# A transformer block on one core: the attention's last product split into three fp32r products, with new instruction orders

## The reference, cut to what matters

```python
x  = L0_attn_x                                   # (8, 1024, 256) fp32, 8 batches
xn = layernorm(x)
# attention without softmax, 16 heads of depth 16
q = elu(xn @ Wq + bq) + 1 ;  k = elu(xn @ Wk + bk) + 1 ;  v = xn @ Wv + bv
k = k / sqrt(sum(k * k, head) + EPS)
attn = (q @ k.T) @ v                             # per head
a = layernorm(xn + attn @ Wo + bo) * gamma + beta
# feed-forward: three blocks with dequantised 4-bit weights and a low-rank addition
h = xn
for blk in range(3):
    y = gelu(layernorm(h @ W[2 * blk].T + b) * g + be)
    h = y @ W[2 * blk + 1].T + b + h
out = x + a + h
```

## Time and profile before

| | |
|---|---|
| median of 3 runs | 626.99 us (626.99 to 627.79) |
| profiled execution, its own time | 627.22 us |
| its span, first to last instruction | 625.5 us |
| TensorE busy | 597.2 us, 95% |
| VectorE busy | 489.4 us, 78% |
| ScalarE busy | 447.2 us, 71% |
| GpSimd busy | 377.6 us, 60% |
| granted TensorE clock, mean | 0.998 |

### The profile page before, as it was taken

One profiled execution on the slowest core, in us unless ns is written; L12 is line 12 of the kernel. 1 busy time (PEld: TensorE's weight loads), 2 busy tenths in 40 slices (PEclk: granted clock), 3 DMA queues, 4 the chain that ended last, 5 costly groups with the idle time before them and its releaser, 6 DMA issues.

```text
span 625.5 us, 10360 instructions
## 1 busy us (share of the span) xinstructions
PE 597.2 (95%) x3365; PEld 508.9 (81%) x3365; DVE 489.4 (78%) x1084; ACT 447.2 (71%) x699; POOL 377.6 (60%) x361
## 2 busy tenths in 40 slices
PE   7999999999998999989999999989999899999996
PEld 7887889878897788968798688977889687987885
DVE  3578679796897868888797968978688887976687
ACT  3367778677778597686796777785976867967752
POOL 3565666366655765466763666557654567626665
PEclk9999999999999999999999999999999999999999
DMA  8103000500004000320005000050003200040001
GB/s 256 42 9 129 0 1 35 168 2 2 0 35 168 0 0 0 116 85 0 0 0 201 0 0 0 34 168 0 0 0 124 78 0 0 0 136 0 2 1 68
DMA packets 11460, 29.01 MB, mean 46 GB/s; under 512 B 2592, under 2 KB 4272, under 8 KB 11440
## 3 DMA queue, kind: packets, MB, share of 16 engines
q1 hardware_dynamic: 10960, 28.35, 13.4%
q10 hardware_dynamic: 480, 0.41, 0.3%
HBM read 20.37 MB, written 8.39 MB: 46 GB/s over the span
## 4 chain that ended last, share of the span: by engine, by line
PE 64%; ACT 14%; POOL 8%; issue 7%; DVE 6%; DMA 1%; POOLq 0%; DVEq 0%; ACTq 0%
PE bank L1469 17%; PE bank L1475 8%; PE bank L1596 8%; PE bank L1640 6%; PE bank L1585 6%; ACT fw L630 5%; PE bank L1542 4%; PE bank L1561 3%; ACT gh L635 3%; POOL gl L262 2%; PE bank L1552 2%; PE bank L1569 2%; PE bank L1529 2%; ACT L630 2%; POOL XNB L412 2%
## 5 line engine op out<-in xcount | busy, mean ns | idle before, releaser
L262 POOL TENSOR_TENSOR gl<-fw,gh 128x512 fp32r<-128x512 f32 x80 | 104.6, 1320 | 74.6 <-ACT gh L635 74.5
L620 ACT ACTIVATE fw<-bank,b1c 128x512 f32<-128x512 f32 x96 | 62.2, 685 | 57.3 <-PE bank L1475 57.1
L417 POOL TENSOR_TENSOR sqs<-fw 128x512 f32<-128x512 f32 x48 | 62.6, 1303 | 63.6 <-ACT fw L620 63.2
L953 DVE SCALAR_TENSOR_TENSOR fw<-bank,b1c,rb 128x512 f32<-128x512 f32 x96 | 68.2, 744 | 18.7 <-ACT rb L626 18.7
L392 POOL TENSOR_TENSOR rsf<-vef,neghalf 128x4 f32<-128x4 f32 x48 | 49.5, 1032 | 52.0 <-DVE vef L944 51.1
L630 ACT ACTIVATE fw<-fw,vec 128x512 f32<-128x512 f32 x96 | 74.1, 808 | 7.1 <-DVE fw L953 5.9
L267 POOL TENSOR_TENSOR hTl<-hT,hTh 128x512 fp32r<-128x512 f32 x40 | 54.5, 1379 | 14.8 <-ACT hTh L639 14.4
L1596 PE MATMUL bank<-K,XN 128*128 128x256 f32 x256 | 60.7, 379 | 0.0
L1640 PE MATMUL bank<-M,qT 128*128 128x256 f32 x256 | 59.0, 379 | 0.0
L635 ACT ACTIVATE gh<-fw 128x512 fp32r<-128x512 f32 x96 | 56.8, 620 | 0.5
L392 POOL TENSOR_TENSOR rs<-ve,neghalf 128x2 f32<-128x2 f32 (+1 forms) x48 | 39.0, 816 | 23.6 <-DVE ve L1041 13.9
(11 more groups left out here) (155 smaller groups left out, 1586.9 us busy)
## 6 DMA issues: line engine op xcount, KB each, us to landing
X<-in_L_attn_x_dram SPq DMA_DIRECT2D x16, 512.0 KB, 6.0
RES<-in_L_attn_x_dram SPq DMA_DIRECT2D x16, 512.0 KB, 4.6
out_dram<-RES SPq DMA_DIRECT2D x14, 512.0 KB, 2.7
XNB<-in_L_ffn_qweights_dram SPq DMA_DIRECT2D x2, 512.0 KB, 6.9
out_dram<-RES SPq DMA_DIRECT2D x4, 256.0 KB, 2.1
RES<-in_L_ffn_qweights_dram SPq DMA_DIRECT2D x1, 512.0 KB, 7.6
Y<-in_L_ffn_lora_a_dram ACTq DMA_DIRECT2D x4, 96.0 KB, 5.1
Wp<-in_L_attn_Wk_dram SPq DMA_DIRECT2D x1, 256.0 KB, 5.3
```

What stands on the lines that cost most here:

```text
L262: engine.tensor_tensor(gl[:, h, m, :], fw[:, h, m, :], gh[:, h, m, :].bitcast(F32), ALU.subtract).then_inc(g_low[h][m], 1)
L417: pool.tensor_tensor(sqs[:, h, :], fw[:, h, 0, :], fw[:, h, 1, :], ALU.add).then_inc(sqs_ready[h], 1)
L620: act.activation(fw[:, h, m, :], FB[h][m][:], ACT.Square, bias=b1c[:, m, j:j + 1]).then_inc(sq_ready[h], 1)
L953: dve.scalar_tensor_tensor(fw[:, h, m, :], FB[h][m][:], b1c[:, m, j:j + 1], rb[:, h, :], ALU.add, ALU.mult).then_inc(yn_ready[h], 1)
```

## The change

1. qT becomes qTh and qTl, M becomes Mh and Ml, all fp32r. `q_elu` writes back to eq; the new `q_higher` (ScalarE) rounds eq to qTh, the new `q_lower` (GpSimd) makes qTl. `m_copy` writes Mh, the new `m_lower` (VectorE) makes Ml.
2. `attend` makes, for each row tile, six fp32r products in place of two in fp32, and waits for the low parts of q (q_low) and of M.
3. eq is free for the next `q_exp` of its column only after `q_lower`.
4. Space: the masked lora_b, lbT, moves into the buffers of sqs and eq, so the first `add_squares` waits until the weights' low parts 0 to 2 are made and the first `q_exp` until all are; the row of bv lies in BD in place of M.
5. New orders of all engines' queues and of the PSUM uses, in head, body and tail, and of the first loads.

```diff
+                if at == HEAD:
+                    act.wait_ge(wT_split, NL)
+                if h or at != HEAD:
+                    act.wait_ge(q_low[m], i * 2 + h)
                 act.activation(eq[:, m, :], RB[r][:], ACT.Exp, bias=neg1[:, 0:1]).then_inc(eq_ready, 1)
+            def q_higher(i, h, m):
+                act.wait_ge(q_ready, nth(i, 2 * NC, h * NC + m))
+                act.activation(qTh[m][:, half(h)], eq[:, m, :], ACT.Copy).then_inc(q_high, 1)
...
+            def q_lower(i, h, m):
+                pool.wait_ge(q_high, nth(i, 2 * NC, h * NC + m))
+                pool.tensor_tensor(qTl[m][:, half(h)], eq[:, m, :], qTh[m][:, half(h)].bitcast(F32), ALU.subtract
+                                   ).then_inc(q_low[m], 1)
...
             def add_squares(i, h, j):
+                if isinstance(i, int) and i == 0 and j == 0:
+                    pool.wait_ge(wT_split, 3)
...
-                dve.scalar_tensor_tensor(qT[m][:, half(h)], eq[:, m, :], 1.0, RB[r][:], ALU.min, ALU.max
+                dve.scalar_tensor_tensor(eq[:, m, :], eq[:, m, :], 1.0, RB[r][:], ALU.min, ALU.max
                                          ).then_inc(q_ready, 1)
+            def m_lower(i, at):
+                r, n = rotating(i, ("m",), at)
+                dve.wait_ge(m_high, nth(i, 1, 0))
+                dve.tensor_tensor(Ml[:].rearrange("p c d -> p (c d)"), RB[r][:],
+                                  Mh[:].rearrange("p c d -> p (c d)").bitcast(F32), ALU.subtract).then_inc(m_ready, 1)
...
             def attend(i, p, at):
                 r = take(i, ("out", p), at)
-                pe.wait_ge(q_ready, nth(i, 2 * NC, p // 2 * NC + NC - 1))
+                for m in range(NC):
+                    pe.wait_ge(q_low[m], nth(i, 2, p // 2))
                 pe.wait_ge(m_ready, nth(i, 1, 0))
+                pairs = [(q, w, c) for q, w in ((qTl, Mh), (qTh, Ml), (qTh, Mh)) for c in range(NC)]
                 for t in range(2):
-                    for c in range(NC):
-                        ins = pe.matmul(RB[r][:, t * D:(t + 1) * D], qT[c][:, (2 * p + t) * P:(2 * p + t + 1) * P],
-                                        M[:, c, :], start=(c == 0), stop=(c == NC - 1))
+                    for n, (q, w, c) in enumerate(pairs):
+                        ins = pe.matmul(RB[r][:, t * D:(t + 1) * D], q[c][:, (2 * p + t) * P:(2 * p + t + 1) * P],
+                                        w[:, c, :], start=(n == 0), stop=(n == len(pairs) - 1))
```

Of the new orders in the loop's body, those that the prediction speaks of, written short (behind a # the place in the queue):

```diff
 # GpSimd
+                q_lower(i, 0, 0)            # between add_squares(i, 0, 1) and add_squares(i, 1, 1)
+                q_lower(i, 1, 0)            # between ffn_root(i, 0, 1) and ffn_root(i, 1, 1)
+                q_lower(i, 0, 1)            # behind g_lower(i, 0, 1, 1)
+                q_lower(i, 1, 1)            # behind ffn_root(i, 0, 2)
-                base_xn(i, 0..3)            # behind ffn_root(1,0), ffn_root(0,1), h_lower(0,1,1), add_squares(1,2)
+                base_xn(i, 0..3)            # behind add_squares(0,0), add_squares(1,0), ffn_root(1,0), ffn_root(1,1)
 # TensorE
                 second_high(i, 1, 1, BODY)
+                make_m(i, BODY)
                 second_low(i, 1, 1)
-                make_m(i, BODY)
 # VectorE
                 q_elu(i, 1, 0, BODY)
+                k_hat(i, 2)
                 k_hat(i, 3)
                 ffn_var(i, 1, 1, BODY)
...
                 ffn_residual(i, 1, 1, 0, BODY)
+                m_lower(i, BODY)
                 ffn_residual(i, 1, 1, 1, BODY)
...
+                att_result(i, 0, BODY)
                 xt_lower(i + 1, 0, 0, BODY)
-                att_result(i, 0, BODY)
 # ScalarE
                 gelu(i, 1, 0, 0)
-                gelu(i, 1, 0, 1)
                 gelu(i, 0, 0, 1)
                 g_higher(i, 0, 0, 1)
+                gelu(i, 1, 0, 1)
...
+                m_copy(i, BODY)
                 q_exp(i, 1, 1, BODY)
-                m_copy(i, BODY)
```

More of the change, by code:

```diff
@@ L455, in head @@
                 dequantise(3)
-                qk_lower(1)
                 dequantise(4)
                 base_xn(0, 0, HEAD)
+                dequantise(5)
                 add_squares(0, 0, 0)
-                dequantise(5)
                 ffn_root(0, 0, 0)
+                qk_lower(1)
+                add_squares(0, 1, 0)
                 base_xn(0, 1, HEAD)
-                base_xn(0, 2, HEAD)
-                add_squares(0, 1, 0)
                 ffn_root(0, 1, 0)
@@ L473, in head @@
                 add_squares(0, 0, 1)
+                q_lower(0, 0, 0)
                 add_squares(0, 1, 1)
@@ L476, in head @@
                 ln1_root(1, 0)
+                q_lower(0, 0, 1)
                 ffn_root(0, 1, 1)
+                base_xn(0, 2, HEAD)
                 base_xn(0, 3, HEAD)
@@ L481, in head @@
                 g_lower(pool, 0, 1, 1, 1)
+                q_lower(0, 1, 0)
                 h_lower(pool, 0, 0, 1, 1)
@@ L484, in head @@
                 add_squares(0, 0, 2)
+                q_lower(0, 1, 1)
+                ffn_root(0, 0, 2)
                 ln2_root(0, 0)
-                ffn_root(0, 0, 2)
                 ln2_root(0, 1)
@@ L539, in tail @@
                 add_squares(i, 1, 0)
+                base_xn(i, 0, TAIL)
                 ffn_root(i, 1, 0)
+                base_xn(i, 1, TAIL)
                 g_lower(pool, i, 0, 0, 0)
@@ L547, in tail @@
                 h_lower(pool, i, 1, 0, 1)
+                q_lower(i, 0, 0)
                 add_squares(i, 0, 1)
-                base_xn(i, 0, TAIL)
+                add_squares(i, 1, 1)
                 ffn_root(i, 0, 1)
-                add_squares(i, 1, 1)
                 ffn_root(i, 1, 1)
+                q_lower(i, 1, 0)
+                base_xn(i, 2, TAIL)
                 g_lower(pool, i, 0, 1, 1)
+                q_lower(i, 0, 1)
                 g_lower(pool, i, 1, 1, 0)
                 g_lower(pool, i, 1, 1, 1)
+                base_xn(i, 3, TAIL)
                 h_lower(pool, i, 0, 1, 1)
-                base_xn(i, 1, TAIL)
+                q_lower(i, 1, 1)
                 add_squares(i, 0, 2)
-                base_xn(i, 2, TAIL)
                 ln2_root(i, 0)
@@ L563, in tail @@
                 ln2_root(i, 1)
-                base_xn(i, 3, TAIL)
                 ffn_root(i, 1, 2)
@@ L764, in head @@
                 ln1_normalise(1, 1, HEAD)
+                q_higher(0, 1, 1)
                 square(0, 1, 2, 0, HEAD)
@@ L806, in body @@
                 h_higher(i, 0, 0, 1)
-                q_exp(i, 0, 1, BODY)
+                q_higher(i, 0, 0)
                 h_higher(i, 1, 0, 0)
@@ L810, in body @@
                 square(i, 0, 1, 0, BODY)
-                q_exp(i, 1, 0, BODY)
                 square(i, 0, 1, 1, BODY)
+                q_exp(i, 0, 1, BODY)
                 square(i, 1, 1, 0, BODY)
                 square(i, 1, 1, 1, BODY)
+                q_exp(i, 1, 0, BODY)
+                q_higher(i, 0, 1)
+                q_higher(i, 1, 0)
                 rb_copy(i, 0, 1, BODY)
@@ L835, in body @@
                 xt_copy(i + 1, 0, 0, BODY)
+                q_higher(i, 1, 1)
                 square(i, 1, 2, 0, BODY)
@@ L1253, in head @@
                 ffn_residual(0, 1, 1, 0, HEAD)
+                m_lower(0, HEAD)
                 ffn_residual(0, 1, 1, 1, HEAD)
                 xt_lower(1, 0, 0, HEAD)
+                h_lower(dve, 0, 1, 1, 0)
                 h_lower(dve, 0, 1, 1, 1)
-                h_lower(dve, 0, 1, 1, 0)
+                q_elu(0, 1, 1, HEAD)
                 att_y(0, 0, HEAD)
@@ L1378, in tail @@
                 k_hat(i, 2)
+                k_hat(i, 3)
+                ffn_var(i, 1, 1, TAIL)
                 ffn_normalise(i, 0, 1, 0, TAIL)
-                ffn_var(i, 1, 1, TAIL)
-                k_hat(i, 3)
                 ffn_normalise(i, 0, 1, 1, TAIL)
@@ L1388, in tail @@
                 ffn_residual(i, 0, 1, 1, TAIL)
+                h_lower(dve, i, 0, 1, 0)
+                q_elu(i, 1, 1, TAIL)
                 ffn_residual(i, 1, 1, 0, TAIL)
                 ffn_residual(i, 1, 1, 1, TAIL)
-                h_lower(dve, i, 0, 1, 0)
-                q_elu(i, 1, 1, TAIL)
+                m_lower(i, TAIL)
                 h_lower(dve, i, 1, 1, 0)
@@ L1823, in head @@
                 spread_rstd(0, 0, 2, HEAD)
+                attend(0, 3, HEAD)
                 attend(0, 2, HEAD)
-                attend(0, 3, HEAD)
                 turn_squares(0, 1, 2, HEAD)
-                rows_state(0, 0)
+                rows_state(0, 1)
                 xt(1, 0, 1, HEAD)
-                rows_state(0, 1)
                 rows_high(0, 1, HEAD)
@@ L1897, in body @@
                 turn_squares(i, 1, 2, BODY)
+                rows_state(i, 0)
+                xt(i + 1, 0, 1, BODY)
                 attend(i, 3, BODY)
[L1899 to L1900 removed]
                 spread_rstd(i, 1, 2, BODY)
```

268 lines of the change are left out of this document (135 added, 133 removed), and 18 rows, old and new, of tables (BODY_USES, HEAD_USES, TAIL_USES).

## The result

The changed kernel takes 632.4 us (median of 4 runs, 632.38 to 632.55) against 627.28 us for the kernel before on the same chip: ratio 1.0081, 95% interval 1.0068 to 1.0094. The forecast was 624.9 us, faster, with a range from 619.5 to 628.5. The sign is wrong, and the range misses the time by 3.9 us.

A forecast was written before the change was run, and what follows sets the result against it. Bound: TensorE nearly full, with a VectorE chain setting block 2 and the attention. Gains of 0.9 (loop), 0.45 (last batch) and 0.7 us (head), 2.05 us, take 627.22 to 625.2, by run median 624.9 us; range 619.5 to 628.5.

The forecast's parts named there:

- The price on TensorE: One attend falls from 1.725 to 1.43 us; 32 attends spare TensorE 9.4 us, 1.18 us a batch.
- C is a chain through VectorE: C, 233.5 to 255.0 (block 2 and the attention), is set by VectorE, with TensorE kept full by fillers.
- The forecast waits: TensorE would wait about 0.6 us before the turn of squares (0,2), and newly before spread_rstd(1,2) or rows_high(0).
- rivals 1 and 2: TensorE's saving pays in full, 617.6 us, chance 0.12; or it pays in part, 620 to 623 us, chance 0.10.
- the VectorE chain 240.88 to 250.63: VectorE from spread_rstd(1,2)'s preceding copy to xt_lower(0,1): same instructions and order, still 9.75 us; 0.15 us a batch gained.
- A lock, weighed: GpSimd and VectorE share ports, so every q_lower can stop a K or Y operation; one K lost 1.01 us.
- rival 3: Slower by the lock in B: blocked k_hat delays spread_rstd(1,1); 627 to 628.1 us, or 634 for two; chance 0.17.
- B: Stretch 204.8 to 233.5, rest of block 0 and block 1: TensorE has no idle time; forecast to keep 28.7 us.
- the 0.84 us of slack: Time between the forecast end of the root of (1,1) and spread_rstd(1,1), which takes it at 220.67.
- The additions: 32 q_higher, 32 q_lower and 8 m_lower fit beside other work; put at nothing, 5 us a batch without cover.
- Head: Before the loop: a wait goes under fillers and Wq lands sooner; 0.7 us gained, between loss 1.5 and gain 3.
- Last batch: Ends on VectorE, which waits for attend(0); one or two shorter attends count, 0.295 or 0.59 us, taken as 0.45.

The follow-up runs named there:

- experiment 1: Changed kernel plus GpSimd waits, in body and last batch, that start block 2's first-half low part only after att_result(1); 627.15 us, ratio 0.9994.
- Experiment 4: Changed kernel with 20 products instead of 12 in the last attend of each loop batch; 627.25 us, ratio 0.9997.
- experiment 5: Kernel of experiment 1 without q_lower and m_lower, high parts multiplied instead, same number of products; 627.07 us, ratio 0.9995.
- kernel 9: kernel 7 plus a GpSimd wait that holds the low part of block 0's second half until rk is ready; 624.62 us, ratio 0.9955.
- kernel 7: Kernel of experiment 1 with ScalarE making the two gh of block 0's second half before the exp of q; 630.75 us, ratio 1.0056.

## Why the prediction was wrong, step by step

- **The price on TensorE** was right: an attend takes 1.42 us where 1.43 was forecast (from 240.79 to 242.21 is one), and the records of all attends cover 50.3 us instead of 59.0. TensorE's busy time as a whole fell by 5.8 us, not by the 8 that the prediction gave as a sign; why is left open.
- **"C is a chain through VectorE", and it starts where it did**: right, 240.91 against 240.88. The forecast waits came as written, 0.65 us before the turn and a new one of 0.48 us before spread_rstd(1,2). So TensorE's saving does not pay, and rivals 1 and 2 were rightly low.
- **The step that failed** is "the VectorE chain 240.88 to 250.63 has the same instructions in the same order after the change", from which its length was taken as fixed. The instructions are the same, but their durations depend on what GpSimd does beside them: the chain took 10.8 us in place of 9.75, all of it one RES operation of 1.53 us in place of 0.48. The same paragraph says that TensorE comes to spread_rstd(1,2) earlier, and does not ask what that triggers: rb's copy, gh, gl, and gl beside RES. Forecast -0.15 us a batch, measured +0.83. With the collision out (experiment 1) a batch takes 73.18 us (from 108.51 to 547.58 over six), 0.17 above the kernel before, so the gain of 0.15 is not there either: the wait that keeps gl away from RES also makes it later. In its trace the first products with gl start when the second gl is done (177.82 in the second batch; its last shown wait before that ends at 172.77). Experiment 4 agrees: there gl starts 0.21 us behind the second RES operation and not 0.56, and a batch takes 72.96 us, 0.05 below the kernel before.
- **"A lock, weighed", and rival 3** had the mechanism and the size (about 1.0 us a case), but the wrong place. In B k_hat(2) and k_hat(3) start ahead of q_lower(1,0) (216.51 against 217.33) and take 1.29 us together, unharmed; it is q_lower that becomes longer (1.59 us). One other K operation of each batch takes 0.93 us, beside the sum of squares, and the 0.84 us of slack held: B took 28.7 us. The mean of all K, 814 ns after 745 before, comes in the main from two in the last batch (1.62 and 1.43 us). Its price, a stall of 1.0 us less what slack there is, is also what C lost: 0.8 us a batch. By the Trainium skill (SBUF — State Buffer, section "SBUF: two separate sides") whichever of the two starts first holds the shared ports for its whole instruction. The traces agree: with GpSimd's gl 0.14 us behind the start of RES the pair takes 0.88 us, and gl takes 1.50 us in place of 1.30; with gl 0.04 us ahead RES stands for 1.05 us. I had priced the added q_lower by that rule and not the moved gl.
- **The additions** at nothing: right (experiment 5), though q_lower is longer than the row it was taken from: 1484 ns on average against 1320.
- **Head**: 0.7 us, measured 0.7 (108.92 to 108.19). The number is luckier than it looks: with the new head that start lay between 107.68 and 108.85 in ten executions, with the old one between 108.92 and 109.19 in three.
- **Last batch**: forecast -0.45 us, measured +0.9. It has the same collision (RES of 1.91 us for two, at 614.60, with gl at 614.29). With the wait of experiment 1 it takes 78.3 us instead of 79.4, so 1.0 us was the collision, and of the forecast gain 0.2 us was there.

The sum as it should have been: -0.7 us for the head, +0.83 in each of six batches, +0.9 at the end, so +5.1 us.

## What to carry to other kernels

Before pricing a saving, list what the shortened instruction triggers through every queue, and hold each of those new starts against the neighbouring operations on VectorE and GpSimd: here two rows stood 0.14 us apart in the right order, and a shift of 0.2 us cost 0.8 us a batch. In a profile of two versions look first for operations that nobody touched and whose longest time has changed; the mean blurs it (477 to 592 ns), the median and the longest show it (477 median, 1534 longest). And where such a pair lies on the path that sets the end, a wait on GpSimd that fixes its order is cheap: it gave 5.3 us in experiment 1 and 6.1 us in kernel 9.

## What was not expected of the hardware

- A small operation can be blocked as well as a large one. ve<-mv, 128x2 elements with one tensor input, takes 0.17 us alone and took 1.22 us at 253.53, while GpSimd ran gl. What is lost does not go by its own size but by what is left of GpSimd's instruction, by the records 0.14 to 0.20 us less than that: guess_sq of kernel 7 (0.29 us alone) starts at 127.27 beside a gl that ends at 128.50 and loses 1.09 of 1.23 us; RES at 248.27 loses 1.05 of 1.25.
- VectorE operations with an input in a bank were not stretched beside the same gl, however large, in any of the thirteen traces. All instances in the changed kernel, least, median and longest ns, first one with an input in a bank, then two whose tensors all lie in SBUF:

```profile
L1121 DVE TENSOR_TENSOR xTl<-bank,xTh x32: 674/681/693, 18.4 to 556.5; 128x512 fp32r<-128x512 f32 x32
...
L1088 DVE TENSOR_SCALAR ve<-mv x32: 169/170/1220, 91.1 to 621.6; 128x2 f32<-128x2 f32 x32
...
L1043 DVE TENSOR_TENSOR K<-K,rk x32: 673/684/1698, 53.1 to 587.4; 128x512 f32<-128x512 f32 x32
```

- An fp32 product of 128x256 costs TensorE 431 ns in a row and the three-fold fp32r form 3 x 119 ns, so the split is cheaper on TensorE by a sixth, and no kernel here turned that into time.
